# One run of the tile pipeline over all four units of a two-layer mixture-of-experts kernel

## The chip, the cores and the metric

The kernel runs on one core of a Trainium2 chip. The metric is the device time of one execution in microseconds (us), lower is better; three executions of the kernel before took 990.3, 990.66 and 993.0 us, so its time is 990.66 us.

## The reference, cut to what matters

Two images of 128 channels and 64 x 64 pixels pass through two layers. Each layer mixes pixels within an image first and then sends every pixel (a token of 128 numbers, 4096 per image) to two of eight experts.

```
x = x + _L0_conv_ref(_ln_c(x), ...)      # depthwise lines, softmax gate per channel
t = _to_tokens(x)
t = t + _L0_ffn_ref(_ln_t(t), ...)       # top-2 of 8 experts: 128 -> 512 -> gelu -> 128
x = _from_tokens(t, x)
x = x + _L1_conv_ref(_ln_c(x), ...)      # max pools of 7 sizes, weighted by a score per channel
t = _to_tokens(x)
t = t + _L1_ffn_ref(_ln_t(t), ...)       # top-2 of 8 experts again, exact gelu
x = _from_tokens(t, x)
```

So the second layer's mixing of an image needs the first layer's expert outputs of that whole image, and its routing needs that mixing.

## The kernel before, in words

**Units and tiles.** A unit is one layer of one image: unit 0 and 1 are layer 0 of image 0 and 1, unit 2 and 3 are layer 1 of the same images. Each unit has 8192 token-expert pairs, sorted into 36 tiles (`TILES`): 28 of 256 slots that belong to one expert each, and 8 whose two halves of 128 slots may have different experts (the last tile has one half). That makes 71 halves and 43 weight loads a unit (`LOADS`).

**One tile.** POOL gathers its rows from `xn_rows` in DRAM with an indirect DMA per half (`gather`, L509). PE turns them (`turn_x`), multiplies by the expert's first matrix (`up`), ACT applies gelu (`activate`), PE multiplies by the second matrix (`down`), ACT adds the bias (`copy_y`), PE turns back (`turn_y`), ACT copies (`copy_rows`), and POOL scatters the rows to `y_rows` with an indirect DMA per half (`scatter`, L519). SP loads the weights. Rows in and rows out have rings of five buffers.

**Steps.** Every engine walks the tiles of a unit with `tile_steps` (L172). At step j of a unit PE turns tile j+1, does `up` of j, `down` of j-1 and `turn_y` of j-2; ACT follows with the same tiles. POOL gathers tile j+5 and then scatters tile j-3:

```
if t.has(G_AHEAD):
    if t.at(G_AHEAD) == (u + 1, 0):
        pool.wait_ge(s_rows, u + 2)
        pool.wait_ge(s_xn_st[u + 1], 16 * QUARTERS)
    gather(t, G_AHEAD)
if t.s == t.last + 1 and u + 1 < UNITS:
    begin(u + 1, range(G_FIRST))
if t.has(-S_BEHIND) and t.at(-S_BEHIND)[1] < TILES - 1:
    scatter(t, -S_BEHIND)
if t.has(-2) and t.at(-2)[1] == TILES - 1:
    scatter(t, -2)
```

Engines run in program order, so what follows a waiting instruction in one engine's program waits with it.

**Runs.** `RUNS` (L66) joins units into runs. `Tile.has` (L124) says whether a tile at a distance d lies in the same run. Within a run the steps go on over the border between units; at the end of a run there are two more steps (36 and 37), in which PE and ACT finish the last tiles and POOL calls `begin` (L529) for the next unit at step 36: it waits for that unit's row lists (`s_rows`) and its normalised rows in DRAM (`s_xn_st`), and gathers tiles 0 and 1. Tiles 2 to 4 are gathered at the start of the next unit.

**The rest of the work** is put between the steps by a table, `WHEN` (L86), with a step for each action of each unit. During unit 1 it holds the mixing of image 0 and the routing of unit 2 (`mixing(0, ...)`), during unit 2 the mixing of image 1 and the routing of unit 3. For unit 1 the row turns and logits of the routing stand at step 28, the normalised rows are written by ACT at steps 30 to 33, the inversion of the sort (`route_invert` on PE) stands at step 33, and SP stores the normalised rows at step 33 (`store_normalised`, L424). For unit 2 the same actions stand at 25, 27 to 30, 30 and 30. VectorE has no steps; its program is `combine(b)`, `mix(b)`, `route(2 + b)` for image 0 and then image 1 (L1328). `combine(b)` adds the expert outputs, which SP loads (`load_outputs`, L430) when all scatters of the unit have landed. `route` ends with the weight list (`tile_experts`, L1152, semaphore `s_experts`) and, after PE's inversion, with the row lists (L1205, `s_rows`).

**Weights on SP.** At step j `load_weights` (L408) issues loads up to six ahead of those of tile j, no further than the end of the run (`end`, L449); the first load of a unit waits for that unit's `s_experts`. What `WHEN` puts at a step is issued before the loads of that step.

Of the kernel before, what the change touches and what calls it, by code (L numbers as in the profile page):

```python
# [62 lines left out]
S_BEHIND = 3  # L63
G_FIRST = 2

RUNS = [(0, 1), (2, 3)]  # L66
BY_SCALAR = [(3, 7), (1, 4, 7)]
BY_VECTOR = sum(GROUPS - len(groups) for groups in BY_SCALAR)
AFTER_UP, AFTER_DOWN = 0.3, 0.6
# [44 lines left out]
class Tile:  # L114

    def __init__(self, unit, j):
        self.s = unit * TILES + j
        run = next(r for r in RUNS if unit in r)
        self.first, self.last = run[0] * TILES, (run[-1] + 1) * TILES - 1
# [66 lines left out]
def begins_run(u):  # L186
    return any(u == r[0] for r in RUNS)


def ends_run(u):  # L190
    return any(u == r[-1] for r in RUNS)

# [12 lines left out]
def build(nc, x, x_tokens, experts, first, later, rows, out):  # L205
    with ExitStack() as ctx:
# [198 lines left out]
        def _(sp):  # L405
# [42 lines left out]
            def weights(u):  # L448
                end = LOADS * (next(r[-1] for r in RUNS if u in r) + 1)  # L449

                def step(t, mid):
                    if t.has():
                        load_weights(min(end, t.load(t.parts() - 1) + 1 + W_AHEAD))
                tile_steps(u, step, plan(u, route_store=store_normalised, outputs=load_outputs, last_store=store_image))
# [922 lines left out]
```

How the kernel before makes its waits and increments, by code:

```python
    def wait(self, back=0):  # L110
        self.eng.wait_ge(self.sem, self.n - back)
# [284 lines left out]
        def banks_read(eng, n):  # L396
            for i in range(2):
                eng.wait_ge(s_freed[i], (n + 1 - i) // 2 + 1)
# [4 lines left out]
        @block.sync  # L404
# [3 lines left out]
            def load_weights(upto):  # L408
                while loads[0] < upto:
                    n = loads[0]
                    unit, i = divmod(n, LOADS)
                    layer, b = divmod(unit, IMAGES)
                    if i == 0:
                        sp.wait_ge(s_experts, unit + 1)
                    if n >= W_RING:
                        sp.wait_ge(s_y_sb, tile_of_load(n - W_RING) + 1)
                    e = sp.value_load(tile_expert[b][0:1, bass.ds(i, 1)], min_val=0, max_val=EXPERTS - 1)
                    w = n % W_RING
                    sp.dma_start(expert[:, w, :], experts[layer, bass.ds(e, 1)].rearrange("a p n -> (a p) n")) \
                        .then_inc(s_w[w], 16)
                    loads[0] += 1
# [1 line left out]
            def store_normalised(u):  # L424
                for q in range(QUARTERS):
                    sp.wait_ge(s_xn, u * QUARTERS + q + 1)
                    sp.dma_start(xn_rows[u].rearrange("(p t) c -> p t c", t=BLOCKS)[:, quarter(q), :],
                                 work_tok[0][:, quarter(q), :]).then_inc(s_xn_st[u], 16)
# [36 lines left out]
            for u in range(UNITS):  # L465
                weights(u)
            sp.wait_ge(s_done, 16 * sum(PIECES[u] for u in range(UNITS - IMAGES, UNITS)))
```

## Time and profile before

| what | value |
|---|---|
| time, median of three executions | 990.66 us |
| the profiled execution, its own time | 989.66 us |
| its span, first to last instruction | 986.8 us |
| busy: PE, PEld, DVE, ACT, POOL | 758.5, 656.6, 555.5, 520.6, 608.4 us |
| granted TensorE clock, mean over the span | 0.884 |
| indirect DMAs on POOL (gathers, scatters) | 284 and 284, 1062 and 1065 ns each |

The shares of busy time are means over stages that have different limits. The stages can be found by their lines: unit 1's last scatter is issued at 557 us, the mixing of image 1 on VectorE follows it and ends at 698 us, and from 758 to 963 us POOL issues indirect DMAs without a break. "Idle before" in a row is the time in which the engine did nothing before that row, and the name behind the arrow is what ended it.

### The profile page before, as it was taken

Reading aid. Unit: us, or ns where it says so; the run is one execution under the profiler, and the core shown is the slowest. Engines: PE = TensorE matmul, PEld = TensorE weight load, DVE = VectorE, ACT = ScalarE, POOL = GpSimd, SP = SyncE. Lnnn points to the kernel's source line nnn. Section 1 sums busy time; section 2 is a strip of 40 time slices with the busy share of each in tenths; the row PEclk is TensorE's granted clock in tenths of the full one; section 3 lists DMA queues with packets and bytes.
Section 4 is the critical chain, followed back from the end, with each engine's and each line's share of the span. In section 5 each row is a group of like instructions: output and inputs, shape, how many; then the busy total and the mean of one; then the engine's idle time right before and its main releaser. Section 6 shows DMA issues by size and latency. Waiting matters only on the chain.

```text
span 986.8 us, 14530 instructions
## 1 busy us (share of the span) xinstructions
PE 758.5 (77%) x4233; PEld 656.6 (67%) x4233; DVE 555.5 (56%) x1262; ACT 520.6 (53%) x1407; POOL 608.4 (62%) x597
## 2 busy tenths in 40 slices
PE   0766249999988798975789499976689977988760
PEld 0535238988887586864788387865679866776760
DVE  7967953263500198999867198999985004100005
ACT  1602427475565465653177376653287754555644
POOL 1000057777777777888632777888754777777760
PEclk9886569999999989999589699998699999999985
DMA  9000255455578483544136773543147856656537
GB/s 356 5 0 1 85 204 160 133 176 162 198 238 286 120 308 128 175 149 129 43 106 227 236 257 123 179 150 126 41 119 237 287 193 220 202 160 239 181 101 255
DMA packets 56861, 165.23 MB, mean 167 GB/s; under 512 B 13888, under 2 KB 13901, under 8 KB 56528
## 3 DMA queue, kind: packets, MB, share of 16 engines
q1 hardware_dynamic: 38608, 128.87, 38.5%
q0 software_dynamic: 18176, 35.44, 12.0%
q8 instruction: 35, 0.57, 0.2%
q14 instruction: 42, 0.34, 0.1%
HBM read 134.89 MB, written 31.20 MB: 168 GB/s over the span
## 4 chain that ended last, share of the span: by engine, by line
DVE 32%; PE 31%; POOL 16%; issue 8%; DMA 6%; ACT 5%; SPq 1%; POOLq 0%; DVEq 0%; ACTq 0%
PE h_ps L787 9%; POOL xg L515 8%; PE yT_ps L800 8%; POOL y_rows L524 8%; DVE state L1290 6%; DVE work L1276 5%; DVE work L1271 5%; DVE tok L1240 4%; PE acc_ps L739 4%; DMA xg<-xn_rows,tile_rows 3%; PE turn_ps L722 3%; PE acc_ps L759 3%; DVE work L1284 2%; DMA work<-y_rows 2%; DVE work L986 2%
## 5 line engine op out<-in xcount | busy, mean ns | idle before, releaser
L515 POOL DMA_INDIRECT xg<-xn_rows,tile_rows x284 | 301.5, 1062 | 226.7 <-DVEq L1206 123.8
L524 POOL DMA_INDIRECT y_rows<-yr,tile_rows x284 | 302.4, 1065 | 127.7 <-issue 82.3
L787 PE MATMUL h_ps<-xT,expert 128*128 128x256 f32 (+1 forms) x1376 | 295.3, 365 | 6.8 <-ACT hT L600 5.5
L600 ACT ACTIVATE hT<-h_ps,expert 128x256 f32<-128x256 f32 (+1 forms) x688 | 250.3, 442 | 72.0 <-PE h_ps L787 71.7
L800 PE MATMUL yT_ps<-hT,expert 128*128 128x256 f32 (+1 forms) x1376 | 278.8, 350 | 1.8 <-ACT yT L611 1.8
L787 PEld LDWEIGHTS h_ps<-xT,expert 128*128 128x128 f32 x1376 | 235.3, 205 | 29.3 <-issue 6.6
L800 PEld LDWEIGHTS yT_ps<-hT,expert 128*128 128x128 f32 x1376 | 233.7, 197 | 27.8 <-ACT yT L611 2.2
L1240 DVE SCALAR_TENSOR_TENSOR tok<-work,share,tok 128x128 f32<-128x128 f32 x224 | 62.3, 348 | 293.0 <-DMA work<-y_rows 292.3
L611 ACT ACTIVATE yT<-yT_ps,expert 128x256 f32<-128x256 f32 (+1 forms) x172 | 72.5, 440 | 116.7 <-PE yT_ps L800 116.6
L776 PE MATMUL xT_ps<-ident,xg 128*128 128x128 f32 x284 | 60.2, 294 | 88.4 <-DMA xg<-xn_rows,tile_rows 85.1
L588 ACT ACTIVATE xT<-xT_ps 128x256 f32<-128x256 f32 x144 | 55.6, 386 | 129.1 <-PE xT_ps L776 129.0
L776 PEld LDWEIGHTS xT_ps<-ident,xg 128*128 128x128 f32 x284 | 34.8, 148 | 100.5 <-DMA xg<-xn_rows,tile_rows 96.3
L1290 DVE SCALAR_TENSOR_TENSOR state<-work,mix_hot,state 128x1344 f32<-128x1344 f32 (+2 forms) x44 | 66.8, 1572 | 0.6
L620 ACT ACTIVATE yr<-yr_ps 128x256 f32<-128x256 f32 x144 | 54.8, 381 | 5.4 <-DMA y_rows<-yr,tile_rows 3.0
L810 PE MATMUL yr_ps<-ident,yT 128*128 128x128 f32 x284 | 54.7, 273 | 2.6 <-ACT yr L620 1.7
L1271 DVE TENSOR_TENSOR work<-work 128x1302 f32<-128x1302 f32 (+4 forms) x38 | 53.6, 1462 | 0.8 <-DVE mix_h L1295 0.5
L1276 DVE TENSOR_TENSOR work<-work 128x1344 f32<-128x1344 f32 (+3 forms) x38 | 53.5, 1461 | 0.5
L810 PEld LDWEIGHTS yr_ps<-ident,yT 128*128 128x128 f32 x284 | 39.0, 141 | 14.4 <-ACT yT L611 3.4
L722 PE MATMUL turn_ps<-ident,tok 128*128 128x128 f32 x128 | 23.1, 337 | 32.3 <-DVE tok L1023 19.5
L722 PE MATMUL turn_ps<-ident,state 128*128 128x128 f32 x128 | 25.5, 374 | 26.1 <-DVE state L1290 22.6
L722 PEld LDWEIGHTS turn_ps<-ident,tok 128*128 128x128 f32 x128 | 18.0, 173 | 35.9 <-DVE tok L1023 21.7
L571 ACT ACTIVATE tok<-turn_ps 128x512 f32<-128x512 f32 x32 | 18.5, 597 | 44.1 <-PE turn_ps L722 44.1
(202 smaller groups left out, 654.3 us busy)
## 6 DMA issues: line engine op xcount, KB each, us to landing
expert<-in_experts SPq DMA_DIRECT2D x172, 514.5 KB, 3.9
work<-y_rows SPq DMA_DIRECT2D x48, 256.0 KB, 6.2
xn_rows<-work SPq DMA_DIRECT2D x16, 512.0 KB, 6.3
xg<-xn_rows,tile_rows POOLq DMA_INDIRECT x284, 3.5
y_rows<-yr,tile_rows POOLq DMA_INDIRECT x284
tok<-in_x_tokens SPq DMA_DIRECT2D x8, 512.0 KB, 7.4
state<-in_x SPq DMA_DIRECT2D x2, 2048.0 KB, 17.4
work<-y_rows SPq DMA_DIRECT2D x8, 512.0 KB, 6.2
```

What stands on the lines that cost most here:

```text
L515: pool.indirect_dma_start(xg[:, s, h, :], None, xn_rows[unit], bass.IndirectOffsetOnAxis(ap=tile_rows[unit % 2][:, 0, at, h:h + 1], axis=0)) \
L524: pool.indirect_dma_start(y_rows[unit], bass.IndirectOffsetOnAxis(ap=tile_rows[unit % 2][:, 1, at, h:h + 1], axis=0), yr[:, s, h, :], None ...
L600: ins = act.activation(hT[:, s, c, cols], h_ps[c // 2][:, c % 2, cols], func, bias=expert[:, t.load(h) % W_RING, BIAS + c:BIAS + c + 1])
L722: mm = pe.transpose(bank[:, k * P:(k + 1) * P], source(t), ident[:])
L776: mm = pe.transpose(xT_ps[:, h * P:(h + 1) * P], xg[:, t.slot(RING, d), h, :], ident[:])
L787: mm = pe.matmul(h_ps[c // 2][:, c % 2, cols], expert[:, t.load(h) % W_RING, c * P:(c + 1) * P], xT[:, t.slot(2), cols], start=True, stop= ...
L800: mm = pe.matmul(yT_ps[:, cols], expert[:, t.load(h, d) % W_RING, HIDDEN + c * P:HIDDEN + (c + 1) * P], hT[:, s, c, cols], start=(c == 0), ...
L810: mm = pe.transpose(yr_ps[:, h, :], yT[:, s, h * P:(h + 1) * P], ident[:])
L1240: ins = dve.scalar_tensor_tensor(tok[b][:, t, :], work_tok[1 + k][:, t, :], share[b][:, k, t:t + 1], tok[b][:, t, :], ALU.mult, ALU.add)
L1271: dve.tensor_tensor(across[:, r, 1:last], pool_in[:, r, 0:edge], pool_in[:, r, 2:SIDE], ALU.max)
L1276: ins = dve.tensor_tensor(pool_in[:, r, :], across[:, r.start - 1:r.stop - 1, :], across[:, r.start + 1:r.stop + 1, :], ALU.max)
L1290: ins = dve.scalar_tensor_tensor(state[b][:, part], work[1][:, part], mix_hot[:, 0, k:k + 1], state[b][:, part], ALU.mult, ALU.add)
```

## The change

One constant: the two runs of two units become one run of four units.

```diff
-RUNS = [(0, 1), (2, 3)]
+RUNS = [(0, 1, 2, 3)]
```

What follows from it in code that stays as it is: unit 1 has no steps 36 and 37 any more. `begin` is called for unit 0 alone. At steps 31 to 35 of unit 1 `t.has(G_AHEAD)` is now true, so POOL waits for `s_rows` and `s_xn_st` of unit 2 at step 31, ahead of the scatter of tile 28, and gathers tiles 0 to 4 of unit 2 at steps 31 to 35, one ahead of each of the scatters of tiles 28 to 32. The scatters of tiles 33 to 35 stand at steps 0 and 1 of unit 2, behind the gathers of its tiles 5 and 6. PE turns tile 0 of unit 2 at step 35 of unit 1. On SP `end` is the end of unit 3, so at step 32 of unit 1 (loads up to unit 1's 37th + 6, one more than its 43) SP issues the first weight load of unit 2, ahead of `store_normalised(2)` at step 33.

## Rows read from the trace of the kernel before

**Rows 1.** The page: shares of the chain that ended last, and one DMA row.

```profile
DVE 32%; PE 31%; POOL 16%; issue 8%; DMA 6%; ACT 5%; SPq 1%; POOLq 0%; DVEq 0%; ACTq 0%
...
xg<-xn_rows,tile_rows POOLq DMA_INDIRECT x284, 3.5
```

**Rows 2.** The chain in order of time: start us, us, what.

```profile
557.23 2.08 DMA y_rows<-yr,tile_rows
...
592.13 8.47 DVE work L986 x32
```

**Rows 3.** PE's instructions in order of time: start, us, what, idle before.

```profile
474.50 3.77 PE L722 MATMUL turn_ps<-ident,state 128*128 128x128 f32 x16 [10.77 <-DVE state L1290]
...
494.98 0.67 PE L776 MATMUL xT_ps<-ident,xg 128*128 128x128 f32 x2
...
530.33 4.42 PE L759 MATMUL acc_ps<-work 128*128 128x144 bf16 x32
...
578.69 1.04 PE L722 MATMUL turn_ps<-ident,tok 128*128 128x128 f32 x8
...
597.75 1.04 PE L722 MATMUL turn_ps<-ident,work 128*128 128x128 f32 x8
...
698.26 3.77 PE L722 MATMUL turn_ps<-ident,state 128*128 128x128 f32 x16 [11.87 <-DVE state L1290]
...
712.56 0.64 PE L776 MATMUL xT_ps<-ident,xg 128*128 128x128 f32 x2
```

**Rows 4.** POOL in order of time, unit 1's end: start, us, what, idle before.

```profile
505.99 0.98 POOL L515 DMA_INDIRECT xg<-xn_rows,tile_rows  x1 [0.30 <-issue]
...
515.42 0.97 POOL L524 DMA_INDIRECT y_rows<-yr,tile_rows  x1 [5.63 <-ACT yr L620]
...
547.01 0.99 POOL L515 DMA_INDIRECT xg<-xn_rows,tile_rows  x1 [0.30 <-issue]
...
557.23 0.97 POOL L524 DMA_INDIRECT y_rows<-yr,tile_rows  x1 [0.30 <-issue]
```

**Rows 5.** DVE in order of time: weight list, row lists, first combine of unit 1.

```profile
532.31 0.18 DVE L1163 CAST tile_expert<-tile_e 128x43 int32<-128x43 f32 x1
...
536.04 0.20 DVE L1205 TENSOR_SCALAR tile_rows<-tile_rows 128x72 uint32<-128x72 uint32 x1
...
563.48 2.37 DVE L1240 SCALAR_TENSOR_TENSOR tok<-work,share,tok 128x128 f32<-128x128 f32 x8 [23.62 <-DMA work<-y_rows]
```

**Rows 6.** ACT in order of time: a bias copy, the last copy of mix_norm.

```profile
527.41 0.74 ACT L611 ACTIVATE yT<-yT_ps,expert 128x128 f32<-128x128 f32 x2
...
603.95 0.20 ACT L578 ACTIVATION_READ_ACCUMULATOR work<-turn_ps 128x1 f32 x1
```

**Rows 7.** SP's issues of unit 2's stores and a load before them; the stores' landing.

```profile
528.88 0.33 SPq L420 DMA_DIRECT2D expert<-in_experts  x1
529.26 0.43 SPq L427 DMA_DIRECT2D xn_rows<-work  x1
...
531.51 1.52 SPq L427 DMA_DIRECT2D xn_rows<-work  x1
...
DMA to landing us min/median/max: 5.1/6.9/7.9
```

**Rows 8.** The border of units 2 and 3: last store and landing; POOL.

```profile
747.52 1.69 SPq L427 DMA_DIRECT2D xn_rows<-work  x1
...
DMA to landing us min/median/max: 6.6/8.3/9.9
...
758.22 0.98 POOL L515 DMA_INDIRECT xg<-xn_rows,tile_rows  x1 [9.75 <-PE xT_ps L776]
...
794.39 0.97 POOL L524 DMA_INDIRECT y_rows<-yr,tile_rows  x1 [0.30 <-issue]
```

**Rows 9.** PE by stretches: busy (count), granted clock, DMA share, GB/s.

```profile
488.00:492.00 4.00, 4.00 (x22) 0.50 0.21 54
...
704.00:708.00 4.00, 4.00 (x28) 0.72 0.16 49
```

## The prediction

> **What bounds the kernel now.** I read the page's shares of the chain first. No engine owns it: VectorE has 32%, PE 31%, POOL 16% [rows 1]. So the question is which engine ends last at each place, and above all at the border of unit 1 and unit 2, where the edit works. The chain in order of time shows the order there: unit 1's last scatter lands, SP loads its outputs, VectorE combines them, mixes image 1 and normalises on the way [rows 2], and PE, which has waited 11.87 us for the mixed state, goes on with unit 2's step 25 at 698.26 [rows 3]. So from the last scatter of unit 1 to step 25 of unit 2 the bound is a chain through VectorE. The tiles of unit 2 run beside it with 11.87 us to spare. Whatever delays unit 1's last scatter delays that chain; whatever brings unit 2's tiles earlier only makes PE wait longer at step 25.
>
> Behind step 25 follow unit 3's routing, its normalised rows and the border of units 2 and 3. From the first gather of unit 3 at 758.22 [rows 8] POOL issues until 963 us, and the outputs follow. All of it hangs on that step and moves with it.
>
> **The change part by part.**
>
> *When POOL may pass the new wait.* At step 31 of unit 1 POOL now needs unit 2's row lists and stored rows. In the trace it reaches that point after its last gather of unit 1, at 505.99 + 0.98 = 507.0, and the scatter of tile 27 behind it, and issues the scatter of tile 28 at 515.42 [rows 4]. The row lists are not ready until 536.24 [rows 5]; they wait for PE's inversion, which stands at step 33 and ends at 534.75 [rows 3]. That part of the program stays ahead of the wait: PE, ACT and SP get as far as step 34 with gathers that POOL has issued by step 30, and the copy of tile 32's rows needs only the scatter of tile 27.
>
> *The stores come later.* SP issued the four stores of unit 2's rows between 529.26 and 531.51, the first one 0.38 us behind a weight load at 528.88 [rows 7]. Now the first weight load of unit 2 stands ahead of them, and it waits for unit 2's weight list, which VectorE finishes at 532.49 [rows 5]. From a wait that ends to the issue SP took 0.73 us: ACT's bias copy ended at 528.15 [rows 6], the load began at 528.88. So the load begins at 533.22, the first store 0.38 us later at 533.60, and the last one 2.25 us (531.51 - 529.26) after that, at 535.85. From issue to landing the slowest store took 7.9 us here [rows 7] and 9.9 us at the border of units 2 and 3 [rows 8]; I take the middle, 8.9, so the rows are in DRAM at 544.75 and not at 539.4. At the border of units 2 and 3, which is of the new kind already, the first gather began at 758.22, and 747.52 + 9.9 = 757.42 is 0.80 us before it. So POOL starts at 545.55, with 544.55 and 546.55 as bounds. Before, the first gather of unit 2 began at 547.01 [rows 4]. The prefetch thus brings the first gather only 1.5 us earlier.
>
> On the landing the trace and the Trainium skill differ. "DMA: Bandwidth & Descriptors", section "Anatomy of one DMA — SWDGE (gpsimd) path", fits a transfer as 2.0 us plus its bytes at 436 GB/s; for 512 KB that is an estimate of 3.2 us. By it POOL would start near 540 and the total below would be some 5.7 us lower. The rows of 7.9 and 9.9 us, with weight loads in the queue, decide.
>
> *What POOL then has to issue.* Behind the wait stand five gathers, one ahead of each of the scatters of tiles 28 to 32, and then the gathers of tiles 5 and 6 and the scatters of tiles 33 to 35: 7 x 2 gathers, 7 x 2 + 1 scatters, 29 indirect DMAs. The border of units 2 and 3 shows the same 29: from 758.22 to 794.39 + 0.97 = 795.36 is 37.14 us, 1.28 us each, without a gap [rows 8]. Unit 1's tiles 33 to 35 must reach POOL in time: PE's step 35 now starts with tile 0's turn, whose gather is issued by 545.55 + 2.57 and lands 3.5 us later [rows 1], at 551.6; the scatter of tile 33 is the 23rd DMA, due at 545.55 + 22 x 1.28 = 573.7. There is time. So the last scatter ends at 545.55 + 37.14 = 582.7. Before it ended at 557.23 + 0.97 = 558.2 [rows 4]. That is **+24.5 us** (23.5 to 25.5) on the chain. Before, five of these tiles had been scattered while the routing ran, in gaps that now stay empty. Of the 29 DMAs, 14 are gathers that nobody on the chain needs yet.
>
> *What the removed steps 36 and 37 give back.* The drain and refill of PE and ACT lay beside the last scatters and the outputs' loads, which are the chain; removing it is worth nothing while unit 2's tiles have slack. They keep it: PE stood at step 4 at 578.69 and reached the wait at step 25 at 698.26 - 11.87 = 686.39, so 107.7 us. Now step 4 waits for the first combined groups, some 5 us behind the first combine, which was at 563.48 [rows 5] and becomes 588.0. So PE reaches step 25 near 701, and VectorE's state is due near 721: the wait grows to some 20 us.
>
> *A little back at the mixing.* PE turned the normalised groups at 597.75, 19.06 us after step 4 [rows 3], while VectorE had begun them at 592.13 [rows 2]; ACT's last copy ended at 604.15 [rows 6]. With PE 24.1 us behind the first combine at step 8, and VectorE's first normalised group 29.7 us behind it, PE now waits there for VectorE, and ACT's last copy comes about 1.6 us behind the last group, 592.13 + 8.47 + 1.6 = 602.2 on the old scale. **-1.9 us** (0 to -2.1).
>
> *TensorE's clock at step 25.* Behind the wait stand two halves of turns and logits, on the chain. After the wait of 11.87 us they took 712.56 - 698.26 = 14.30 us, at a granted clock of about 0.72 [rows 3, 9]. The same work for unit 2, in unit 1's steps, after a wait of 10.77 us, took 494.98 - 474.50 = 20.48 us, at 0.50, the level of 1.2 GHz, though PE was busy in all of it [rows 3, 9]. Both waits are alike, so a longer one may cost anything between 0 and +6.18 us against now; I take the middle, **+3.1 us**. The Trainium skill ("TensorE: Matmul & The Clock Gate", Part 1) has sustained work win the full clock back soon, by which the term would be 0; the stretch at 0.50 with PE fully busy says otherwise here.
>
> *Sum.* 24.5 - 1.9 + 3.1 = +25.7 us on the profiled execution's own 989.66 us: 1015.4 us. The median of the runs shown is 1.0 us above that execution, so 1016 us.
>
> **Rivals.**
>
> A. *The stores are no obstacle*: they land as early as before, or SP's order matters less, and POOL starts when the row lists are there. Earliest start 536.24 + about 0.8 (as behind the landed stores above) = 537.0, last scatter 574.2, +16.0, and with -1.9 and 0 to 6.2 of clock +14 to +20: 1004 to 1011 us. For it: the sequence of SP is read from the code, not seen. Against: at the border of units 2 and 3 the first gather came 0.80 us behind the landing of the stores [rows 8], so it was these that held it.
>
> B. *The gathers really come early, and the kernel gets faster.* Its place is POOL's idle time before 547: if POOL passed the wait before it needs the scatter of tile 28, at 515, the gathers of tiles 0 and 1 (4 x 1.28 = 5.1 us), which now stand ahead of the scatters of tiles 33 to 35, would be gone from there, the last scatter would end at 553.1 and the chain be 5.1 us shorter: 985.5 us. It decides from the point where the row lists are ready within the idle time; the gain is zero when POOL is held 5.1 us beyond what the old order held it. Rows 5 put the row lists at 536.24, 21 us too late, and nothing in the edit moves the routing.
>
> C. *The delay is swallowed*: the chain through VectorE is not rigid, and the later outputs eat into waits elsewhere. The wait of 23.62 us that VectorE has ahead of its first combine [rows 5] is on the chain and grows; the only other wait seen, PE's 11.87 us, is PE's and not VectorE's. Time about 991 us.
>
> D. *The gathers and outputs collide more*: the tiles of unit 2 are further when the outputs load, PE's clock falls in more places. Up to 1024 us.
>
> **How the numbers follow.** Forecast 0.70: its own range is 21.4 to 31.7 us (23.5 - 2.1 + 0; 25.5 - 0 + 6.2), 1012 to 1022 us on the median. A 0.15, B 0.05, C 0.04, D 0.06. The range from 1004 to 1022 us holds the forecast and A and leaves out B, C and D. About 0.3% (3 us) is what a measurement of this kernel can tell from no change: faster is B, same is C, slower all the rest, 0.91.
>
> **What the changed profile would show.** POOL idle from about 510 to 545, at a gather and not at a scatter; then 29 indirect DMAs without a break in the order gather, scatter; SP's four stores between 533 and 537, behind a weight load; the last scatter of unit 1 at 582; VectorE's wait ahead of its combine up from 23.6 to about 48 us; PE's wait at unit 2's step 25 near 20 us. The forecast is wrong if unit 2's first gathers are issued before 536, or if PE at step 25 waits for gathered rows and not for VectorE.

## The result and the profile after

The change made the kernel slower: 1010.59 us (median of 6) against 990.48 us, ratio 1.0208 with a 95% interval of 1.0175 to 1.0241. The forecast was 1016 us, 1004 to 1022.

Single executions of one kernel spread more than the forecast said: the kernel before took 979 to 997 us in the executions beside the experiments. So the times below are medians with their intervals, and where a profile is compared, it is by stretches that start at an event both executions share: the end of unit 2's row lists (L1205).

POOL of the changed kernel at the border of units 1 and 2, in order of time (start, us, what, idle before), answers to [rows 4]:

```profile
547.42 0.99 POOL L515 DMA_INDIRECT xg<-xn_rows,tile_rows  x1 [33.19 <-issue]
...
583.61 0.97 POOL L524 DMA_INDIRECT y_rows<-yr,tile_rows  x1 [0.30 <-issue]
```

POOL stands still for 33.19 us with the scatters of tiles 28 to 32 behind the wait, in a stretch in which it used to issue them in gaps of 5 to 9 us. Then come the 29 DMAs, 37.16 us long, and the single scatter of the last half tile ends at 584.58. The first gather of unit 2 starts at 547.42, 6.8 us behind the row lists (540.62); before it was 10.8 us behind them (547.01 - 536.24). So the gathers stand among the last scatters, and the first is only 4.0 us earlier.

VectorE of the changed kernel (weight list, row lists, first combine of unit 1), answers to [rows 5]:

```profile
536.54 0.18 DVE L1163 CAST tile_expert<-tile_e 128x43 int32<-128x43 f32 x1
...
540.42 0.20 DVE L1205 TENSOR_SCALAR tile_rows<-tile_rows 128x72 uint32<-128x72 uint32 x1
...
589.47 2.31 DVE L1240 SCALAR_TENSOR_TENSOR tok<-work,share,tok 128x128 f32<-128x128 f32 x8 [45.23 <-DMA work<-y_rows]
```

SP of the changed kernel, and the landing of its four stores, answers to [rows 7]:

```profile
537.54 0.33 SPq L420 DMA_DIRECT2D expert<-in_experts  x1
537.91 3.65 SPq L427 DMA_DIRECT2D xn_rows<-work  x4
...
DMA to landing us min/median/max: 5.1/6.1/6.6
```

VectorE waits 45.23 us ahead of its combine where it waited 23.62: 21.6 us more. The stores follow the weight load, and that follows the weight list (536.72) by 0.82 us. By the trace the last store was issued at 540.24 and landed at 546.66, 0.76 us ahead of POOL's first gather; that was 6.0 us behind the row lists, where before it was 3.1 (539.38).

PE of the changed kernel, answers to [rows 3]:

```profile
591.84 1.12 PE L722 MATMUL turn_ps<-ident,tok 128*128 128x128 f32 x4 [15.09 <-DVE tok L1240]
...
620.95 0.73 PE L722 MATMUL turn_ps<-ident,work 128*128 128x128 f32 x4 [3.75 <-DVE work L986]
...
723.69 3.72 PE L722 MATMUL turn_ps<-ident,state 128*128 128x128 f32 x16 [13.52 <-DVE state L1290]
...
738.05 0.67 PE L776 MATMUL xT_ps<-ident,xg 128*128 128x128 f32 x2
```

PE now waits at step 4, 15.09 us, and at step 8, and still 13.52 us at step 25. At step 25 unit 2's tiles had 11.87 us to spare before and have a little more now.

From the row lists' end to PE's step 25 it was 162.0 us before (698.26 - 536.24) and is 183.1 us now (723.69 - 540.62): **+21.1 us**, which is the timed difference of 20.1 us within the spread. The row lists themselves were 4.4 us later in this execution, ahead of anything that the change touches (the routing of unit 1 already ended 4.3 us later), and behind step 25 the execution was 2.4 us shorter; neither is counted to the change.

### The profile page after: what moved, and what is told of

It is laid out like the page before. It is cut to its first block, busy times and chain, and to the rows that moved or that the text cites. A ratio compares the mean times of both kernels' runs of the same rounds, so it can differ in the third digit from the quotient of the medians.

```text
span 1009.8 us, 14530 instructions
## 1 busy us (share of the span) xinstructions
PE 766.1 (76%) x4233; PEld 660.8 (65%) x4233; DVE 554.9 (55%) x1262; ACT 521.8 (52%) x1407; POOL 608.6 (60%) x597
## 3 DMA queue, kind: packets, MB, share of 16 engines
q0 software_dynamic: 18176, 35.44, 11.9%
## 4 chain that ended last, share of the span: by engine, by line
PE 34%; DVE 31%; POOL 13%; issue 8%; DMA 8%; ACT 4%; SPq 0%; POOLq 0%; DVEq 0%; ACTq 0%
PE h_ps L787 10%; PE yT_ps L800 9%; POOL xg L515 7%; POOL y_rows L524 6%; DVE state L1290 6%; DVE work L1276 5%; DVE work L1271 5%; DMA xg<-xn_rows,tile_rows 4%; PE turn_ps L722 4%; DVE tok L1240 4%; PE acc_ps L739 4%; PE acc_ps L759 3%; DVE work L1284 2%; DMA work<-y_rows 2%; PE xT_ps L776 1%
## 5 line engine op out<-in xcount | busy, mean ns | idle before, releaser
L800 PE MATMUL yT_ps<-hT,expert 128*128 128x256 f32 (+1 forms) x1376 | 275.8, 347 | 1.8 <-ACT yT L611 1.8
```

Of the source, the lines that this page charges most:

```text
L800: mm = pe.matmul(yT_ps[:, cols], expert[:, t.load(h, d) % W_RING, HIDDEN + c * P:HIDDEN + (c + 1) * P], hT[:, s, c, cols], start=(c == 0), ...
```

## The experiments

All kernels below are the kernel before or the changed one with the edit that is shown. The table has what each profile shows at the border of units 1 and 2, in us from the end of the row lists: POOL's first gather of unit 2, the end of unit 1's last scatter, VectorE's mixing score (L1300), and PE's start on step 25. The last two columns are the median time and its ratio to the kernel before, as that ran beside the same experiment (medians of 987.9 to 990.5 us), with its interval. So ratios compare rows better than times do. One execution of each kernel was profiled; those of "scatters first" (989.4 us) and "one run, timed" (979.5 us) were the fastest of theirs.

```
                       gather  scatter   score  step 25   time   ratio (95%)
before                  10.8     22.0     73.8   162.0
the change               6.8     44.0     94.9   183.1   1010.6  1.021 (1.018 to 1.024)
scatters first          10.8     29.3     80.1   168.3    997.4  1.011 (1.008 to 1.015)
store first              0.3     37.8     87.9   176.1   1001.7  1.014 (1.008 to 1.019)
early route              5.9     43.1     92.3   180.5   1012.0  1.022 (1.017 to 1.028)
begin last              17.2     16.9     74.7   162.9    993.5  1.004 (1.001 to 1.008)
five before             10.8     29.4     79.2   167.4    998.1  1.012 (1.003 to 1.021)
begin early              0.9     17.2     68.1   156.3    985.5  0.999 (0.995 to 1.003)
drain first             10.8     22.0     73.5   161.7    986.2  1.002 (0.998 to 1.006)
both                     0.3     17.0     68.6   156.8    988.6  1.002 (0.998 to 1.006)
drained and retimed      0.3     16.9     68.5   156.7    979.2  0.989 (0.984 to 0.993)
one run, timed           0.6     19.4     69.7   157.9    989.5  1.000 (0.997 to 1.003)
```

From score to step 25 it is 88.2 us in every row. Whatever reaches the score reaches step 25 undiminished: VectorE's mixing is rigid, and rival C has no place to swallow anything there.

Behind step 25 the rows are not alike. The next table has PE's wait ahead of step 25, the stretch from step 25 to the end of unit 3's row lists, and in it PE's busy time and mean granted clock.

```
                        wait   stretch   PE busy   clock
before                 11.87     53.2      48.7     0.87
the change             13.52     53.0      48.4     0.87
scatters first         13.44     53.0      48.4     0.87
store first            13.54     53.1      48.5     0.87
early route            11.79     56.1      51.5     0.82
begin last             11.85     58.5      54.0     0.77
five before            12.07     59.0      54.5     0.78
begin early            12.14     61.5      56.9     0.73
drain first            13.55     53.4      48.8     0.86
both                   12.11     58.6      54.0     0.77
drained and retimed    12.12     61.4      56.9     0.73
one run, timed         13.54     53.0      48.5     0.87
```

PE is idle for 4.5 us of the stretch in every row and issues the same 301 matmuls; what differs is how long they take, at a granted clock of 0.73 to 0.87. From unit 3's row lists to the end it is 232 to 235 us in all rows. So the kernel before and the changed one can be compared, as both have the short stretch, but a gain or loss of some 5 us at step 25 can be covered or doubled behind it. Whether the long stretch belongs to a kernel or to an execution, one profile each does not show.

**Scatters first** (the change, with unit 1's scatters 28 to 32 no longer behind the wait):

```diff
+at = t.at()
+late = (1, TILES - G_AHEAD) <= at <= (2, 1)
-if t.has(G_AHEAD):
+if t.has(G_AHEAD) and not late:
     ...
     gather(t, G_AHEAD)
 ...
+if at == (1, TILES - 1):
+    pool.wait_ge(s_rows, u + 2)
+    pool.wait_ge(s_xn_st[u + 1], 16 * QUARTERS)
+    for d in range(1, 4):
+        gather(t, d)
+if at == (2, 1):
+    for d in range(2, G_AHEAD + 1):
+        gather(t, d)
```

> One run of four units as in the change, but at the border of units 1 and 2 POOL issues the scatters of tiles 28 to 32 without waiting; the wait and the gathers of unit 2's tiles 0 to 2 stand behind the scatter of tile 32, and the gathers of tiles 3 to 6 behind the last scatter. Theory (the loss is unit 1's last scatters, held behind the wait and behind 14 gathers): five of the eight tiles are out by 547 as before the change, 6 gathers and 5 scatters stay, but tiles 33 to 35 now leave PE between the first steps of unit 2 and wait for its gathers' landing, so the last scatter ends some 9 us later than before the change instead of 22, and the time is about 997 us (994 to 1001). Rival 1 (the loss is PE's and ACT's mixed border steps, or the clock, and not POOL's order): the time stays at 1008 to 1012. Rival 2 (the gathers ahead are the whole loss): 990 to 992.

The time is 997.4 us and the last scatter 7.3 us later than before, not 22: by the profile POOL's wait and order carry two thirds of the loss (21.1 us at step 25 become 6.3), by the ratios, 1.011 against 1.021, about half. The rest is what was expected of the mixed border. PE in that kernel (in its kernel.py lines behind the edit are numbered 10 higher):

```profile
547.62 0.69 PE L786 MATMUL xT_ps<-ident,xg 128*128 128x128 f32 x2 [8.20 <-DMA xg<-xn_rows,tile_rows]
...
559.63 0.27 PE L820 MATMUL yr_ps<-ident,yT 128*128 128x128 f32 x1
```

PE stands 8.20 us at tile 0 of unit 2 before it may finish unit 1's last tiles, and turns the last of them at 559.63, 26.6 us behind the row lists (533.0); before it was 548.18, 11.9 us behind them:

```profile
548.18 0.33 PE L810 MATMUL yr_ps<-ident,yT 128*128 128x128 f32 x1 [0.46 <-ACT yT L611]
```

**Store first** (the change, SP's stores one step earlier):

```diff
-    return steps + [(rows[-1], "route_store", u)]
+    return steps + [(rows[-1] - (b == 0), "route_store", u)]
```

> The change, but SP issues the stores of unit 2's normalised rows one step earlier, ahead of the first weight load of unit 2. Theory (these stores hold POOL's wait, and they are late by SP's order): the last store is issued some 4 us earlier, POOL's first gather of unit 2 starts 3 to 4 us earlier, and the time is 1006 to 1008 us; the rest of the loss stays. Rival (POOL's wait ends with the row lists, SP's order is no part of it): 1010 to 1011 us, and POOL starts as late as in the change.

SP issues the four stores from 523.44 to 530.74, and the last one lands at 534.60, ahead of the row lists (535.44). POOL's first gather of unit 2 and unit 1's last scatter:

```profile
535.77 0.99 POOL L515 DMA_INDIRECT xg<-xn_rows,tile_rows  x1 [26.75 <-DVEq L1206]
...
572.28 0.97 POOL L524 DMA_INDIRECT y_rows<-yr,tile_rows  x1 [0.30 <-issue]
```

The wait now ends with the row lists (released by L1206), 0.3 us behind them instead of 6.8. The gain at the last scatter is 6.2 us, nearly twice the 3 to 4 expected: the stores moved past a second weight load too, which the changed kernel issues at 533.34 behind a wait for a tile's copy. In time it is 7 us by the ratios (1.014 against 1.021); that the 1001.7 us lie below the expected span comes in part from the kernel before, whose median was 2.3 us lower beside this experiment. So 6 of the 22 us were stores that stood behind two weight loads. The longer run had put only one of them there: the stores landed 3.1 us behind the row lists before the change and 6.0 us with it, so some 3 us are the change's own.

**Early route** (the change, unit 2's routing at the steps that unit 3's has):

```diff
-mixing(0, read=3, state=(6, 7, 8, 9), norm=11, route=(28, 28), slots=30.3, rows=(30, 31, 31.6, 33),
-       invert=(33, 33, 33, 33)),
+mixing(0, read=3, state=(6, 7, 8, 9), norm=11, route=(25, 25), slots=27.3, rows=(27, 28, 28.6, 30),
+       invert=(30, 30, 30, 30)),
```

> The change, with the routing of unit 2 put at the earlier steps of unit 1 that unit 3's routing has in unit 2 (turns at 25, inversion and stores at 30 instead of 28 and 33). Theory (VectorE's state, not the step, decides when the routing starts; the row lists come as late as before, but fewer of unit 1's tiles are done by then): POOL still stands at step 31 until the stores have landed, PE waits three tiles longer at step 25, and the border takes what that of units 2 and 3 takes, 97 to 103 us from the first turn to the last scatter instead of 105.6: 1002 to 1009 us, far from 990.5. Rival (the change lacks only a retimed table; with it the gathers really come ahead): below 990 us.

PE at the start of unit 2's routing:

```profile
479.83 3.77 PE L722 MATMUL turn_ps<-ident,state 128*128 128x128 f32 x16 [29.16 <-DVE state L1290]
```

PE waits 29.16 us at step 25 for a state that comes no sooner. The border took 103.3 us (479.83 to 583.11), the upper end of what was expected, but the time of 1012.0 us is 3 us above it. An earlier step in the table did not make the row lists earlier (540.03 against 540.62), and the rival (below 990) is out.

**Five before** (the kernel before, five tiles gathered ahead of the last three scatters, not two):

```diff
-    begin(u + 1, range(G_FIRST))
+    begin(u + 1, range(G_AHEAD))
 ...
-for d in range(G_FIRST, G_AHEAD):
+for d in range(G_FIRST if u == 0 else G_AHEAD, G_AHEAD):
```

> The kernel before, but at the border of units 1 and 2 POOL gathers five tiles of unit 2 instead of two ahead of unit 1's last three scatters; nothing is waited for earlier. Theory (what stands on POOL ahead of the last scatters is paid on the chain): 6 more gathers of 1.28 us, the last scatter 7.7 us later, less up to 2 us that the mixing gives back as PE's steps come to lie ahead of VectorE: 5.5 to 8 us slower than the kernel before. Rival (the tiles of unit 2, not the scatters, decide; behind the last scatter two gathers more or less cost nothing): no slower than before.

The end of unit 1's scatters on POOL:

```profile
563.63 0.97 POOL L524 DMA_INDIRECT y_rows<-yr,tile_rows  x1 [0.30 <-issue]
```

Six gathers more put the last scatter 7.5 us later (expected 7.7) and step 25 5.5 us later, with no wait and no drain changed. The interval of the time's ratio, 1.012 (1.003 to 1.021), is wide, but all of it is above 1. This isolates the price of a gather ahead of the last scatter: 1.25 us at the scatter, 0.9 us at step 25. The profiled execution lost 5.8 us more in the stretch behind step 25, which is not counted to the gathers.

**Begin last** (the kernel before, no gather ahead of the last scatters):

```diff
-if t.s == t.last + 1 and u + 1 < UNITS:
-    begin(u + 1, range(G_FIRST))
 ...
     scatter(t, -2)
+if t.s == t.last + 2 and u + 1 < UNITS:
+    begin(u + 1, range(G_FIRST))
```

> The kernel before with one edit: at the border of units 1 and 2 the two tiles that POOL gathers ahead of the last three scatters are gathered behind them. Theory (the last scatter of unit 1 is on the chain that sets the end, the first gathers of unit 2 are not): 4 x 1.28 = 5.1 us of POOL leave the chain, the last scatter ends 5 us earlier, the time is 985 to 986.5 us. Rival (unit 2's tiles are the bound, which the change wanted to bring forward): its first tile starts 6 us later, and the time is the same or up to 6 us longer, 990 to 997 us.

The expectation was wrong. The last scatter ended 5.1 us earlier, as expected, and yet the kernel came out 0.4% slower (0.1 to 0.8%). PE at its step 8:

```profile
600.16 1.04 PE L722 MATMUL turn_ps<-ident,work 128*128 128x128 f32 x8
```

VectorE at the same place:

```profile
590.24 8.53 DVE L986 TENSOR_SCALAR work<-tok,rstd,shift 128x128 f32<-128x128 f32 x32
606.66 0.16 DVE L1259 TENSOR_REDUCE gap<-gap_parts 128x1 f32<-128x8 f32 x1 [7.89 <-ACT work L578]
```

The same in the kernel before:

```profile
604.25 0.16 DVE L1259 TENSOR_REDUCE gap<-gap_parts 128x1 f32<-128x8 f32 x1 [3.66 <-ACT work L578]
```

VectorE began to normalise earlier against the row lists than before (52.5 us against 55.9), but PE reached its step 8, where it turns the normalised rows, only at 600.16, and VectorE waited 7.89 us for them, where it had waited 3.66. The mixing needs two things: the last scatter of unit 1 and PE at steps 4 to 8 of unit 2. Before, PE was already the later of the two; taking two gathers away from it cost what the scatter gained, and 0.9 us more at the score and at step 25. That explains why nothing was won. Of the 4 us by which the median is slower it explains 0.9; the profiled execution had the long stretch behind step 25 (5.3 us more), and whether the others had is not shown.

**Begin early** (the kernel before, stores one step earlier as in "store first", and the two gathers ahead of the scatter of tile 31):

```diff
-if t.s == t.last + 1 and u + 1 < UNITS:
+if t.s == t.last - 1 and u + 1 < UNITS:
     begin(u + 1, range(G_FIRST))
```

> The kernel before with two edits: SP stores unit 2's normalised rows one step earlier, and POOL waits for unit 2 and gathers its tiles 0 and 1 two steps earlier, ahead of the scatter of tile 31, where POOL is idle for some 4 us behind the row lists. Theory (both the last scatter of unit 1 and PE's first steps of unit 2 are needed by the mixing): the last scatter ends about 5 us earlier and tile 0 is there 8 us earlier, so 3 to 6 us faster than the kernel before. Rival 1 (POOL's order at the border is worth nothing, the loss of the change came from elsewhere): the same as before. Rival 2 (any gather ahead of a scatter costs): slower by up to 5 us.

POOL's first gather of unit 2 and unit 1's last scatter:

```profile
537.96 0.99 POOL L515 DMA_INDIRECT xg<-xn_rows,tile_rows  x1 [5.56 <-DVEq L1206]
...
553.29 0.97 POOL L524 DMA_INDIRECT y_rows<-yr,tile_rows  x1 [0.30 <-issue]
```

The gathers fall into POOL's idle time right behind the row lists. Both paths get shorter, the last scatter by 4.7 us and step 25 by 5.7 us. In time it is 0.999 (0.995 to 1.003): a gain of up to 5.3 us is within the interval and none is as well, so the 3 to 6 us that were expected are not shown, and up to 5.3 us are not excluded. In the profiled execution the 5.7 us were lost behind step 25, where PE's stretch took 8.3 us more than before at a granted clock of 0.73.

**Drain first** (the kernel before, the other border drained as well):

```diff
-RUNS = [(0, 1), (2, 3)]
+RUNS = [(0,), (1,), (2, 3)]
```

> The opposite of the change at the other border: the kernel before with unit 0 and unit 1 as runs of their own, so that unit 0 is drained and POOL gathers only two of unit 1's tiles ahead of unit 0's last scatters. Theory (combining and mixing image 0 hangs on unit 0's last scatter, as image 1 on unit 1's): ten gathers leave POOL ahead of the last scatter, VectorE starts its combine 8 to 12 us earlier, PE's wait ahead of its step 28 in unit 1 covers the tiles' later start, and the kernel is 6 to 11 us faster. Rival (a drained border costs what the pipeline loses there, which the change was to save at the other border): 4 to 8 us slower.

SP's loads of unit 0's outputs:

```profile
336.13 8.49 SPq L438 DMA_DIRECT2D work<-y_rows  x16
```

This expectation was wrong too: unit 0's last scatter ended at 323.1 instead of 336.3, but SP did not begin to load the outputs before 336.13. `load_outputs` stands at step 3 of unit 1 in SP's program, behind weight loads that wait for tiles. The gain stopped at the next queue.

**Both** together (drain first with begin early):

> Units 0 and 1 drained, POOL's two gathers of the next unit ahead of the third scatter from the last at both drained borders, and the stores one step earlier. Theory: the gains of the two edits add, 9 to 16 us faster than the kernel before. Rival (the earlier chain uncovers the tiles of unit 1 or 2 as the bound): no better than the better of the two alone.

The step 25 of unit 2 was 5.2 us earlier against the row lists as in "begin early", unit 0's border gave nothing, and the time, 1.002 (0.998 to 1.006), did not move: here too the stretch behind step 25 was longer, by 5.4 us. The gains of the two edits did not add, and neither showed.

**Drained and retimed** ("both", and three places of the table moved):

```diff
-mixing(0, read=3, state=(6, 7, 8, 9), norm=11, ...
+mixing(0, read=1, state=(3, 4, 5, 6), norm=8, ...
```

> The kernel with units 0 and 1 drained and POOL's gathers two steps earlier (the two edits that were run together before), and three places of the table for image 0 moved forward: SP loads unit 0's outputs at step 1 of unit 1 instead of 3, the turns of the combined tokens stand at steps 3 to 6 instead of 6 to 9 and those of the normalised ones at 8 instead of 11. Theory (unit 0's last scatter did end 13 us earlier when it was drained, and the gain was lost because SP's program held the outputs' load behind weight loads until PE was at a later tile): the load follows the last scatter, the combine starts 8 to 11 us earlier, and the time is 9 to 15 us below the kernel before. Rival (PE's later start of unit 1's tiles is what held the mixing): no change against the kernel without the three moves.

SP's loads of unit 0's outputs:

```profile
328.37 8.86 SPq L438 DMA_DIRECT2D work<-y_rows  x16
```

VectorE's first combine and the end of its first half of the mixed image 0:

```profile
332.42 2.32 DVE L1240 SCALAR_TENSOR_TENSOR tok<-work,share,tok 128x128 f32<-128x128 f32 x8 [58.32 <-DMA work<-y_rows]
...
464.31 2.48 DVE L1290 SCALAR_TENSOR_TENSOR state<-work,mix_hot,state 128x1024 f32<-128x1024 f32 x2
```

PE's first turn of that state:

```profile
472.67 1.04 PE L722 MATMUL turn_ps<-ident,state 128*128 128x128 f32 x8
```

This is the fastest, and faster than both kernels: 979.2 us, 0.989 (0.984 to 0.993) of the kernel before, some 11 us less, as expected. The load now follows the last scatter (it ended at 327.24, the load began at 328.37), and the combine starts 71.3 us behind unit 1's row lists (261.14) instead of 84.8 (341.81 - 257.03). Part of the gain is lost again: VectorE had the state's first half ready at 466.79, PE came to it at 472.67 without a wait. Here unit 1's tiles have become the bound.

**One run, timed** (one run, stores first, the wait at step 34 with three gathers; `at` and `late` are those of "scatters first"):

```diff
 if t.has(G_AHEAD) and not late:
     ...
+if at == (1, TILES - 2):
+    pool.wait_ge(s_rows, u + 2)
+    pool.wait_ge(s_xn_st[u + 1], 16 * QUARTERS)
+    for d in range(2, 5):
+        gather(t, d)
 ...
+if at == (2, 1):
+    for d in range(2, G_AHEAD + 1):
+        gather(t, d)
```

> One run of four units as in the change, but POOL waits for unit 2 only at step 34, where the row lists become ready, ahead of the scatter of tile 31: gathers of tiles 0 to 2 there, the scatters of tiles 28 to 30 ahead of the wait, the gathers of tiles 3 to 6 behind unit 1's last scatter; SP stores the rows one step earlier. Theory (one run costs nothing by itself; what cost is the wait at step 31 and 14 gathers ahead of the last scatters): the last scatter ends 1 to 2 us earlier against the row lists than before the change, and the time is 986 to 990 us, 2 to 5 us below the kernel before. Rival (PE's and ACT's border steps without a drain delay tiles 33 to 35): 994 to 998 us, as in the run with the scatters first.

The wait ends with the row lists, the last scatter is 2.6 us earlier than before and step 25 4.1 us earlier; the time, 989.5 us, is 1.000 (0.997 to 1.003) of the kernel before. So a single run of all four units can be had without the loss, but it does not measurably gain on the two runs.

## Why the prediction was right

The direction, the cause and the failure of the rivals came out as forecast; the sum was 4.6 us too large (25.7 against 21.1), by three of its terms (2.5 - 1.0 + 3.1).

*When POOL passes the wait.* Forecast 9.3 us behind the row lists (545.55 - 536.24), measured 6.8. SP's order was as read from the code: the last store went out at 540.24 and landed at 546.66, 0.76 us ahead of the gather. The landing was mis-sized: 8.9 us forecast, 6.4 measured, -2.5 us. The estimate from the Trainium skill's fit ("DMA: Bandwidth & Descriptors", "Anatomy of one DMA — SWDGE (gpsimd) path") was 3.2 us; that fit is for DMAs that gpsimd issues, and these stores are issued by SP. With 6.4 us for the last store, the measurement lies between the two, further from the fit. The four stores of the same size at 103 to 112 us, which in the changed kernel stand in the queue with no weight load near them, took 2.6 to 2.7 us; so the 6.4 us are no fixed price of a store.

*The 29 DMAs.* Forecast 37.14 us, measured 37.16. The last scatter came 22.0 us later (44.0 - 22.0). "Store first" shows that 6.2 of them were the stores, some 3 us of them by the load that the change put ahead, and "five before" that a gather in front of the last scatter costs 1.25 us.

*The mixing gives a little back.* Forecast -1.9 us, and from the normalising to the score it was -2.2 us (from 17.88 to 15.70 us), with PE's 3.75 us of wait at step 8 as its sign. But combine and statistics, from the last scatter to the normalising, took 1.3 us longer, as VectorE waited 1.74 us for the second part of the outputs instead of 0.29; so -0.9 us stayed. Of rival D this is what the trace shows on the chain.

*The clock at step 25.* Forecast +3.1 us as a middle between two rows. The stretch took 14.36 us (738.05 - 723.69) against 14.30, both at a mean granted clock of 0.74: nothing. The Trainium skill's rule ("TensorE: Matmul & The Clock Gate", Part 1), by which sustained work wins the clock back, gives the right term here, but not by its way: the clock stayed at 0.71 to 0.72 from 723.7 to 741.7 with PE busy all the time, and the same kernel's stretch at 479 us, 20.5 us long at 0.50, again does not fit it. That this term was nothing is in part luck: in six of the twelve profiled executions PE's work from step 25 to unit 3's row lists took 3 to 8 us longer, and no run shows what decides it.

*PE's wait at step 25* was forecast at some 20 us and was 13.52. The step that failed is the one which moved PE's tiles along rigidly: PE takes 118.3 us from step 4 to its wait (591.84 to 710.17) and not 107.7. It is idle for 6.0 us more, mostly as it waits for VectorE at steps 4 and 8 (2.97 and 3.75 us), and busy for 4.6 us more (100.0 against 95.4) at a mean granted clock of 0.92 against 0.97. It costs nothing, as the wait is still one for VectorE.

Rival A's start (POOL at the row lists) is what "store first" made; it was not the case here. Rival B needed the row lists at 515; they came at 540. What was not foreseen is how near unit 2's tiles stood to being the bound in the kernel before. They had 11.87 us at step 25, but none at step 8, where VectorE already waited 3.66 us for what PE had turned and ACT copied. So the statement that unit 2's tiles run beside the chain with time to spare was wrong there, and "begin last", which followed from it, won nothing.

## What to carry to other kernels

A prefetch that is put into an in-order queue ahead of stores does not only use idle slots: it carries its waits with it, and everything behind it waits too. Before gathering ahead, look when the list to gather by is ready, and whether the last stores in that queue are the start of the next chain; if so, stores first until the list is there, then just as many gathers as the next step needs. In this kernel that took the loss away and did not show a gain. And look for slack at each place where two paths meet, not only at the last one: an edit may be free at one join and not at another, and an earlier result gains nothing until the next queue's program lets it be used.

## What the runs showed of the hardware that was not expected

PE's work right behind a wait of 11 to 14 us differs in length from execution to execution. From the first turn of a mixed state to VectorE's reading of the logits it took 17.4 to 17.7 us in some and 20.7 us in others (once 19.6), for the same work and waits of much the same length: in the kernel before 20.7 for unit 2 and 17.4 for unit 3, in "one run, timed" 17.5 and 17.4, in "begin early" 20.7 and 20.7. The stretch from there to the row lists runs from 36.4 to 41.1 us for unit 2 and from 35.5 to 40.9 us for unit 3. At unit 3 the difference is all PE's busy time, 48.4 to 56.9 us for the same 301 matmuls, at a granted clock of 0.87 to 0.73. Behind waits of 13.4 to 13.6 us the whole stretch took 53.0 to 53.4 us in all five executions, behind 11.8 to 12.1 us it took 56.1 to 61.5 in six of seven; at unit 2's step 25 there is no such order. The kernel before spreads over 18 us: beside the experiments its nine executions under 982 us had a granted clock of 0.890 to 0.901 over the span, its eight above 994 us one of 0.873 to 0.881. What decides on the clock was not tried.
